# Half tiles of the adjacency matrix from tile 30 on: six transfers with rows of 2 KB in place of one with rows of 12 KB

## What is computed

```python
# x (6144, 512), adj (6144, 6144) of 0 and 1 (int32, sparse), W (8, 512, 64), a1 and a2 (8, 64), all float32 but adj
h  = maximum(layernorm(x), 0)
hh = einsum('ni,hif->hnf', h, W)
s1, s2 = einsum('hnf,hf->hn', hh, a1), einsum('hnf,hf->hn', hh, a2)
scores = leaky_relu(s1[:, :, None] + s2[:, None, :], 0.2)
scores = where(adj[None] > 0, scores, -9e15)
out = einsum('hnm,hmf->hnf', softmax(scores, axis=-1), hh)
return x + elu(out.transpose(1, 0, 2).reshape(6144, 512))
```

## Time and profile before

| | |
|---|---|
| median of 3 runs | 812.9 us (811.7 to 812.99) |
| profiled execution | 814.42 us, its span 812.6 us |
| VectorE busy | 687.4 us, 85% |
| TensorE busy | 610.1 us, 75% |
| ScalarE busy | 471.6 us, 58% |
| GpSimd busy | 388.6 us, 48% |
| moved by DMA | 269.51 MB, mean 332 GB/s |

### The profile page before, as it was taken

How to read it: one execution, slowest core, us unless ns; L and a number is a source line. 1 busy time by engine, 2 the same in 40 slices (tenths; PEclk the granted TensorE clock), 3 DMA queues, 4 the chain that set the end, 5 groups by cost and what they waited for, 6 DMA issues and landing times.

```text
span 812.6 us, 9242 instructions
## 1 busy us (share of the span) xinstructions
PE 610.1 (75%) x2182; PEld 357.3 (44%) x2182; DVE 687.4 (85%) x2066; ACT 471.6 (58%) x695; POOL 388.6 (48%) x775
## 2 busy tenths in 40 slices
PE   0698988897688758553886697768878859988874
PEld 0364554454354434342543354444444435554442
DVE  4897998997777677564999799999999988999995
ACT  0647999989999989225565365647453213233322
POOL 4644544442333332227776336447375655757610
PEclk9998999989998997855999698886887869999997
DMA  9956999999999999328999999999996766969852
GB/s 289 424 207 229 339 411 417 417 403 407 422 421 419 420 421 423 150 66 316 407 409 417 406 367 400 413 414 397 410 398 199 263 194 204 297 206 296 288 174 105
DMA packets 65130, 269.51 MB, mean 332 GB/s; under 512 B 12145, under 2 KB 12145, under 8 KB 52786
## 3 DMA queue, kind: packets, MB, share of 16 engines
q1 hardware_dynamic: 45314, 203.12, 63.1%
q0 software_dynamic: 19760, 65.78, 23.6%
HBM read 243.49 MB, written 25.37 MB: 331 GB/s over the span
## 4 chain that ended last, share of the span: by engine, by line
DVE 26%; PE 12%; issue 8%; DMA 6%; POOL 3%; ACT 0%; DVEq 0%; POOLq 0%
DVE nodes L1098 8%; PE psO L1237 7%; DMA nodes<-table,list_column 4%; DVE places L248 4%; PE psO L1243 3%; DVE best L237 3%; DVE agg L1109 2%; DMA nodes<-table,column 2%; POOL nodes L934 2%; DVE to_row L1068 1%; DVE result L1121 1%; POOL nodes L929 1%; PE psC L1223 1%; DVE owner L1032 1%; PE psD L1238 1%
## 5 line engine op out<-in xcount | busy, mean ns | idle before, releaser
L601 PE MATMUL psH<-sb_W,normedT 128*128 128x512 f32 x384 | 225.5, 678 | 0.0
L1237 PE MATMUL psO<-nodes,ident 128*128 128x512 f32 x276 | 183.7, 758 | 43.5 <-issue 39.9
L227 ACT ACTIVATE packed<-adj_rows,eight 128x3072 uint8<-128x3072 int32 x66 | 188.3, 2853 | 0.7
L929 POOL DMA_INDIRECT nodes<-table,column x138 | 135.3, 980 | 85.5 <-PE psD L1244 45.0
L934 POOL DMA_INDIRECT nodes<-table,list_column x109 | 112.5, 1032 | 86.9 <-DVE list_column L1057 56.4
L1098 DVE TENSOR_TENSOR nodes<-nodes,psW 128x2048 f32<-128x2048 f32 (+4 forms) x66 | 138.7, 2142 | 0.0
L1243 PE MATMUL psO<-nodes,to_row 128*128 128x512 f32 x218 | 124.9, 661 | 6.3 <-DVE nodes L1098 6.1
L643 POOL TENSOR_TENSOR sb_node_sum<-sb_node_sum,h_rows 128x512 f32<-128x512 f32 x48 | 61.2, 1275 | 141.6 <-ACT h_rows L566 141.6
L602 PEld LDWEIGHTS psS<-sb_Wa,normedT 128*128 128x128 f32 x384 | 78.6, 205 | 103.5 <-issue 103.5
L248 DVE FIND_INDEX8 places<-best,packed 128x8 uint32<-128x96 f32 (+6 forms) x240 | 109.9, 465 | 0.0
L237 DVE MAX8 best<-packed 128x8 f32<-128x96 f32 (+6 forms) x240 | 102.8, 460 | 0.5 <-ACT packed L227 0.5
(11 more groups left out here) (177 smaller groups left out, 923.3 us busy)
## 6 DMA issues: line engine op xcount, KB each, us to landing
adj_rows<-in_adj_dram SPq DMA_DIRECT2D x66, 1536.0 KB, 10.7
sb_adj_rows<-in_adj_dram SPq DMA_DIRECT2D x30, 1536.0 KB, 14.6
table<-h_rows SPq DMA_DIRECT2D x48, 260.0 KB, 9.0
sb_x_rows<-in_x_dram SPq DMA_DIRECT2D x48, 256.0 KB, 9.2
kept<-in_x_dram SPq DMA_DIRECT2D x19, 512.0 KB, 7.0
out_dram<-result SPq DMA_DIRECT2D x19, 512.0 KB, 4.0
kept<-in_x_dram SPq DMA_DIRECT2D x10, 256.0 KB, 8.8
out_dram<-result SPq DMA_DIRECT2D x10, 256.0 KB, 7.6
```

Of the source, the lines that this page charges most:

```text
L227: nc.scalar.activation(words.bitcast(mybir.dt.uint8), sb["adj_rows"][buffer_of(i)][:], ACT.Square, bias=sb["eight"][:], scale=-17.0, accum ...
L601: nc.tensor.matmul(psH[:, t % 2], normedT[:, t % 2, kc], sb["W"][:, kc], start=(kc == 0), stop=(kc == KC - 1))
L929: nc.gpsimd.indirect_dma_start(out=nodes[:, node_at[u] + i * w.direct + j], out_offset=None, in_=table, in_offset=bass.IndirectOffsetOnAxi ...
L1237: nc.tensor.matmul(psO[:, o, to], sb["ident"][:], nodes[:, n0 + q, 0:HF], start=a, stop=False)
```

## The change

Halves 0 to 59 are loaded as before. Each half from 60 on is loaded by six transfers of 512 columns (rows of 2 KB, 256 KB in all) after one wait, and the count that `pack` waits for is 16 for each of them.

```diff
 def adj_landed(i):
-    return 16 * sum(buffer_of(k) == buffer_of(i) for k in range(i + 1))
+    return 16 * sum(len(pieces(k)) for k in range(i + 1) if buffer_of(k) == buffer_of(i))
+
+
+def pieces(i):
+
+    return [(0, HALF)] if i < 2 * EARLY else [(lo, lo + 512) for lo in range(0, HALF, 512)]
...
-    sp.dma_start(sb["adj_rows"][u][:], adj[t * P:(t + 1) * P, i % 2 * HALF:(i % 2 + 1) * HALF]).then_inc(sb["adj_loaded"][u], 16)
+    for lo, hi in pieces(i):
+        sp.dma_start(sb["adj_rows"][u][:, lo:hi],
+                     adj[t * P:(t + 1) * P, i % 2 * HALF + lo:i % 2 * HALF + hi]).then_inc(sb["adj_loaded"][u], 16)
```

## The result

| | kernel before | the change |
|---|---|---|
| median of four runs, us | 812.3 (811.1 to 813.0) | 826.8 (825.8 to 828.3) |
| span of the profiled execution, us | 812.6 | 824.2 |
| granted TensorE clock, mean of the core | 0.864 | 0.858 |

The change is slower: ratio 1.0187, 95% interval [1.0157, 1.0217], 14.5 us between the medians and 11.6 us between the two spans. The forecast was 817.5 with a range of 807 to 828. So the side was right and the time lay in the range, but the loss is three times the forecast, and that size has to be explained. The traces show only the 11.6 us. In the change the pack is L234 (L227 before), the load L221 (L215) and psW L1015 (L1008).

What follows compares the result with a forecast made beforehand. From 383 to 605 us VectorE and the DMA engines were taken to limit together. Half 95's lateness of 4.6 us, with SP and the scan-stage halves at zero, was added to the 812.9 us median: 817.5 us, range 807 to 828.

Steps and rivals of the forecast that it cites:

- Who goes first: Late half tiles beside gathers: with 2 KB rows gathers get about two thirds of the engines and land in 4 to 5 us.
- the second wait: VectorE's wait for a gather before unit 6, 4.9 us until 459.3 us; forecast to go.
- the first wait: VectorE's wait for a gather before the first unit, 9.6 us until 378.4 us; forecast to shrink by some 4 us.
- a rival: Order does not change: gathers stop about 1.5 us as q1 starts; 4 to 9 us slower; 0.17 together with dear packets.
- The price: A late half as 48 packets of 0.0848 us costs every DMA engine 4.07 us instead of 3.68, 0.39 us more.
- the rival of cheap packets: At 0.0805 us per packet a half costs 0.18 us more: 810.7 us; 808.7 with no price; no separate chance given.
- the dear packets: At 0.090 us per packet, 0.64 us more a half, half 95 is 12.9 us late: 825.8 us; 0.17 with unchanged order.
- The ledger: DMA work from 371.5 us against ScalarE's packs: half 73 +0.1 us net, half 95 4.6 us late, all let through.
- SP: 180 more issues at 0.33 us; queued store and kept load lose at most 1.7 us, used some 27 us later: zero.
- The late halves of the scan stage: Halves 60 to 62 cost 1.2 us of DMA at 308 to 325 us and 5 us of SP: zero.
- What would show it: Signs: DMA share 1.0 with about 3% fewer GB/s, half tiles 12 to 18 us, new pack and psW waits, unchanged shift after 650.

Runs made afterwards that it cites:

- e12: The change, but GpSimd issues unit 15's gathers only once half 88 is packed and unit 16's once half 89 is: 819.4 us, ratio 1.0096.
- e6b: Kernel before, rows of 12 KB, plus an unread load of 128 rows of 1 KB ahead of each late half, four spare regions: 818.2 us, ratio 1.0081.
- e7: The change with the last 256 columns of every late half left out, so a half costs about its old engine time: 814.8 us, ratio 1.0016.
- e2: The change's 2 KB rows issued by two transfers per late half instead of six: 821.2 us, ratio 1.0097 against the kernel before.
- e5: The change with the kept loads issued from ScalarE's queue instead of SP's: 828.7 us, ratio 1.0199 against the kernel before.

## Why the prediction was right on the side and wrong on the size

*Who goes first: right for the gathers, half right for the waits.* In the window 425 to 446 they land after 6.1 to 6.6 us at the median, not 25 (forecast 4 to 6), and the second wait is gone. But the first wait was to shrink by 4 us and shrank by 0.7. When the first half starts, the gathers under way get almost nothing for a while, whether the rows have 2 KB (the change, 371 to 372.5 us) or 12 KB (the kernel before, 372.5 to 374.5):

```profile
q1 hardware_dynamic: 230, 0.41, 76.0%
q0 software_dynamic: 20, 0.07, 16.0%
```

```profile
q1 hardware_dynamic: 71, 0.87, 102.7%
q0 software_dynamic: 1, 0.00, 0.0%
```

The profile of before had shown this, and the prediction used it only for a rival. 3.3 us are missing from the first unit on; the stop of 1.5 us is a part of them, and the rest stays open.

*The price: right.* Window 480 to 483 us of the change has q1 alone, 568 packets of 512 B or more in 48 engine-us (16 engines for 3 us):

```profile
DMA packets 641, 1.16 MB, mean 388 GB/s; under 512 B 73, under 2 KB 73, under 8 KB 641
q1 hardware_dynamic: 640, 1.16, 105.2%
```

48 / (641 - 73) is 0.0845 us a packet, where 0.0848 was forecast. This speaks against the rival of cheap packets. The Trainium skill (DMA: Bandwidth & Descriptors, Why small descriptors are slow) gives a packet three cycles of its own, and 0.0796 was the estimate from them; the trace disagrees with it. The time came out at 826.8, just above the 825.8 of the dear packets, but not for their reason.

*The ledger: this is the step that failed.* Its 4.6 us stand against 14.5. It asked at two deadlines, halves 73 and 95, whether all work issued by then fits in the time since 371.5, and took the lateness at the last one, 4.6 us, for the whole loss. Half 95 was not late at all: it had landed at 622.5 us, near the ledger's 624.8, and its pack at 628.4 waited for nothing. The loss was made in the middle, at halves nobody had asked about: 66 to 69, and 88 and 89. Two things were wrong with the sum. It has no order in it: it counts the gathers of units 15 and 16 as work that may be done at any time, while with short rows they are served ahead of halves 88 and 89, which are needed sooner; e12 holds them back and those 9.4 us go. And lateness is no backlog that can be made up: a half is issued only when a buffer is free, three packs earlier, so the ring can't run ahead and each local loss stays until the end, but for what the kernel before lost itself at unit 6. Hence the losses of separate places add, where the ledger takes one. At half 73 it gave +0.1 net, and the units there stand at +2.7.

*Where the 1.9% comes from.* The price in the old order costs 0.81% (e6b). The turns at the old price, with six transfers, cost 0.16%, with an interval that holds zero (e7). That is 0.97% together, where the change costs 1.87%. The kernel with the change's rows in two transfers costs 0.97% (e2), so the 0.9% that the sum lacks appears only with six transfers and the price at once, and mostly at unit 14. The trace of the kernel before shows little room: half 65 lands at 395.7 and is packed at 398.0, half 89 lands at 560.8 and is packed at 566.1, 2.3 and 5.3 us. That each cost alone stays mostly within this room and all together exceed it in the bursts is the likely reading, and no run shows it. The forecast of 4.6 us was not far from the 5.7 that the price costs alone (818.2 less 812.5), but that is luck: it came from lateness at half 95, which did not happen.

*SP: zero is not borne out.* Kept was to lose at most 1.7 us with 27 in hand; it landed 21.1 us after its issue and was waited for 6.4 us. SP's issues took up to 4.4 us instead of 0.33, so that half 90, free to go after the pack that ended at 562.3, was begun at 566.9. Without the kept wait the loss is the same (e5), so that wait is not what costs. But two transfers in place of six took 0.9% off (e2), so the six transfers were put at nothing too early; how much of it is SP's time no run tells.

*The late halves of the scan stage: zero, right.* The first half of the joint stretch is issued at 368.9 us, where it was 370.0.

*What would show it.* The DMA share stayed full with 4.5% fewer GB/s (404 to 386; 3% forecast), the waits of the pack and of psW appeared, and after unit 15 the shift stays at 11.7 us. Half tiles took up to 28 us (half 89), not 18, which was the sign of the bursts.

## What to carry to other kernels

Where two queues share full DMA engines, look at the row length of their transfers. Here the gathers had 34% of the engines beside rows of 12 KB and 55% beside rows of 2 KB: shorter rows in one queue handed bandwidth to the other, which helps only if the other's data is needed sooner. Look for bursts in the queue that gains, and test the deadline of every transfer that falls into one, not the first and the last: in a ring that cannot run ahead, local losses add. And the parts of a change need not add up: the price alone cost 0.8% and the new order alone 0.2%, both together 1.0% in two transfers and 1.9% in six. So try each part alone and also the whole in another form, before judging any. Rows of 4 or 6 KB cost nothing that can be measured here.

## What was not expected of the hardware

- With transfers of 32 partitions and 12 KB rows, 384 KB each, both queues together moved 249 GB/s (400 to 440 us), where with transfers over 128 partitions and the same rows it was 404 (383 to 605); gathers beside them landed in 41.6 us.
- An issue on SP's queue takes 0.33 us, but up to 4.4 us (5.5 with two transfers per half, 7.2 for a kept load there) in the kernels that queue many short packets.
- When an idle SP queue starts, gathers under way are nearly stopped for 1.5 to 2 us: 20 packets against 230 with rows of 2 KB, 1 against 71 with rows of 12 KB.
